# Attention and FFN block for one core: the order of all engines from attention step 14 on written out, O of four half batches turned into SBUF, O transposed held twice

## What is computed

```python
x = L0_attn_x                                   # (16, 256, 256)
xn = _layernorm(x, axis=-1)
x = x + _L0_attn_ref(xn, w_qkv, w_out) + _L0_ffn_ref(xn, w_gating, w_linear)

# attention: 16 heads of 16, causal
q, k, v = (qkv[:, :, 0], qkv[:, :, 1], qkv[:, :, 2])
scores = jnp.einsum('bqhd,bkhd->bhqk', q / 4, k)
scores = jnp.where(causal_mask[None, None], scores, NEG)
out = jnp.einsum('bhqk,bkhd->bqhd', jax.nn.softmax(scores, axis=-1), v).reshape(b, s, HIDDEN)
return out @ w_out

# FFN: operands cast to float8 e4m3
activations = jax.nn.gelu(_qdot(x, w_gating[0])) * _qdot(x, w_gating[1])
return _qdot(activations, w_linear)
```

## Time and profile before

| | us |
|---|---|
| median of 3 runs | 353.13 |
| lowest, highest | 351.51, 353.25 |
| the profiled execution | 353.16 |
| its span (first to last instruction) | 351.4 |

### The profile page before, as it was taken

One profiled execution on the slowest core, in us unless ns is written; L12 is line 12 of the kernel. 1 busy time (PEld: TensorE's weight loads), 2 busy tenths in 40 slices (PEclk: granted clock), 3 DMA queues, 4 the chain that ended last, 5 costly groups with the idle time before them and its releaser, 6 DMA issues.

```text
span 351.4 us, 9794 instructions
## 1 busy us (share of the span) xinstructions
PE 336.0 (96%) x3514; PEld 256.4 (73%) x3514; DVE 294.4 (84%) x1359; ACT 227.4 (65%) x369; POOL 167.6 (48%) x203
## 2 busy tenths in 40 slices
PE   6899999999999999999999999999999999996996
PEld 6446556666676778788888888888888888884775
DVE  5798898989425787999999999899999999999865
ACT  1585677767655576676667766767667666775470
POOL 4114314422225364456675466664755657557461
PEclk9999999999999999999999999999999999999899
DMA  7949975673238243534528346274364552624011
GB/s 239 351 133 294 268 217 156 142 245 122 78 134 298 94 151 109 199 114 161 181 94 270 115 160 209 100 239 158 118 211 136 199 179 97 213 90 157 2 64 60
DMA packets 46569, 57.59 MB, mean 164 GB/s; under 512 B 2680, under 2 KB 39096, under 8 KB 46520
## 3 DMA queue, kind: packets, MB, share of 16 engines
q1 hardware_dynamic: 46520, 56.96, 50.1%
HBM read 16.78 MB, written 12.58 MB: 84 GB/s over the span
## 4 chain that ended last, share of the span: by engine, by line
PE 81%; DVE 9%; DMA 4%; ACT 2%; issue 2%; SPq 1%; DVEq 0%; ACTq 0%
PE ps L954 13%; PE ps L845 13%; PE ps L932 11%; PE ps L905 9%; PE ps L852 7%; PE ps L832 7%; PE ps L975 6%; PE ps L809 6%; PE ps L815 6%; DVE masked L531 4%; DMA xres<-in_L_attn_x_dram 3%; PE ps L963 2%; PE ps L792 2%; DMA xt_store<-stack 1%; ACT gate L618 1%
## 5 line engine op out<-in xcount | busy, mean ns | idle before, releaser
L531 DVE CUSTOM_DVE_ANT_0 masked<-ps,causal 128x256 bf16<-128x256 f32 (+1 forms) x512 | 148.2, 353 | 17.0 <-PE ps L905 17.0
L663 ACT ACTIVATE arena<-ps 128x1024 f32<-128x1024 f32 x96 | 98.3, 1027 | 54.5 <-PE ps L932 54.2
L366 POOL TENSOR_SCALAR_AFFINE_SELECT arena<-arena 128x512 f32<-128x512 f32 (+1 forms) x96 | 73.8, 790 | 32.6 <-ACT arena L663 32.5
L337 POOL TENSOR_TENSOR qk_part<-w_raw,qk_part 128x512 fp32r<-128x512 f32 x32 | 41.2, 1287 | 52.0 <-ACT qk_part L642 52.0
L618 ACT ACTIVATE gate<-ps 128x512 bf16<-128x512 f32 x64 | 38.4, 603 | 27.9 <-PE ps L809 27.7
L932 PE MATMUL ps<-stack 64*128 64x256 f32 (+1 forms) x512 | 51.2, 300 | 2.3 <-ACT arena L663 2.2
L845 PE MATMUL ps<-xs,wq_part 128*128 128x256 f32 x384 | 52.3, 285 | 0.3 <-ACT w_raw L636 0.3
L954 PE MATMUL ps<-arena,v_aug 128*32 128x256 f32 (+1 forms) x1024 | 49.5, 335 | 1.7 <-DVE o_norm L548 1.7
L905 PE MATMUL ps<-stack 63*128 63x256 f32 (+1 forms) x512 | 47.7, 285 | 2.0 <-DVE row_max L531 1.8
L845 PEld LDWEIGHTS ps<-xs,wq_part 128*128 128x128 f32 x384 | 47.5, 189 | 1.5 <-ACT w_raw L636 0.6
L932 PEld LDWEIGHTS ps<-stack 64*128 64x128 f32 x512 | 35.9, 186 | 15.0 <-issue 5.7
(11 more groups left out here) (64 smaller groups left out, 453.1 us busy)
## 6 DMA issues: line engine op xcount, KB each, us to landing
stack<-qk_part SPq DMA_DIRECT2D x96, 256.0 KB, 2.8
xs<-xt_store SPq DMA_DIRECT2D x16, 512.0 KB, 4.4
xt_store<-xt_part SPq DMA_DIRECT2D x14, 512.0 KB, 4.2
out_dram<-w_raw SPq DMA_DIRECT2D x15, 256.0 KB, 4.4
xres<-in_L_attn_x_dram SPq DMA_DIRECT2D x7, 512.0 KB, 6.7
arena<-in_L_ffn_w_gating_dram SPq DMA_DIRECT2D x2, 1024.0 KB, 10.3
stack<-zeros SPq DMA_DIRECT2D x4, 512.0 KB, 7.6
arena<-in_L_ffn_w_linear_dram SPq DMA_DIRECT2D x1, 1024.0 KB, 14.3
```

Of the source, the lines that this page charges most:

```text
L337: nc.gpsimd.tensor_tensor(qk_part[:, g, QLO:KLO + 1:3, :], qk_raw[:, g, :, :], qk_part[:, g, QHI:KLO, :].bitcast(F32), ALU.subtract).then_ ...
L366: nc.gpsimd.affine_select(diag, diag, pattern=[[0, 1024 // width], [1, P]], compare_op=ALU.is_ge, fill=0.0, base=0, channel_multiplier=-1) ...
L531: last = nc.vector.tensor_tensor_reduce(masked[:, place, i * width:(i + 1) * width], max_ps[:, place, i * width:(i + 1) * width], causal[: ...
L663: nc.scalar.activation(arena[:, n, :, :], exp_banks(b, n), ACT.Exp).then_inc(exp_done, 1)
```

## The change

From step 14 on, no engine's order comes from the loop any more; all of them are written out, instruction group by instruction group. With that come four smaller edits:

- `o_to_rows` of the four half batches (12,1), (13,0), (13,1) and (14,0) writes into SBUF (`o_by_q`, on the place of the FFN's weights `wg8`, done with by then) and not back into the bank; `normalize_o` then reads it there, and the next `times_v` waits only for `o_to_rows` and not for the multiply of `normalize_o`.
- `ot_part` is held twice, by the batch's parity, so `round_ot` waits for a `project_out` two batches back and not one.
- Batch 14's output projection and transposed maxima use the other bank of `misc`.
- `keep_warm` of 4 goes, that of 12 becomes 8 and writes another bank. DVE's last subtraction (L597) comes before `add_x(14)` and not after.

No work is added or removed otherwise. The diff, with the lists of SP, POOL and ACT cut short:

```diff
+        o_by_q = wg8[:, :, :, :].rearrange("p g k n -> p (g k n)").bitcast(F32).rearrange("p (c n) -> p c n", c=2)
         ot_raw = xn[:, 2:4, :]
         o_norm = sb("o_norm", [P, S], F32)
-        ot_part = xt_part[:, :, :, 0:S]
+        ot_part = [xt_part[:, :, :, i * S:(i + 1) * S] for i in range(2)]
...
-            return misc[:, 1, :] if b == B - 1 else misc[:, 1 - c, :]
+            return misc[:, 1, :] if b >= B - 2 else misc[:, 1 - c, :]
-            return exp_ps[:, t, 0:D] if b == B - 1 else misc[:, 0, t * D:(t + 1) * D]
+            return exp_ps[:, t, 0:D] if b == B - 1 else misc[:, int(b == B - 2), t * D:(t + 1) * D]
+        def leaves_bank(b, c):
+            return -7 <= 2 * (b - B) + c <= -4
...
-            for s in range(B + 5):
+            for s in range(B - 2):
...
+            place_max(B - 1, 1)
+            store_y(B - 5)
+            store_y(B - 3)
+            store_y(B - 4)
+            store_y(B - 2)
+            store_y(B - 1)
...
-                nc.gpsimd.tensor_tensor(ot_part[:, 1, c, :], ot_raw[:, c, :], ot_part[:, 0, c, :].bitcast(F32),
+                nc.gpsimd.tensor_tensor(ot_part[b % 2][:, 1, c, :], ot_raw[:, c, :], ot_part[b % 2][:, 0, c, :].bitcast(F32),
...
+            mask(B - 1, 4)
+            mask(B - 1, 5)
+            split_ot(B - 2, 0)
             split_ot(B - 2, 1)
             split_ot(B - 1, 0)
...
+                if leaves_bank(b, c):
+                    dve.wait_ge(o_norm_done, 2 * b + c - 1)
+                nc.vector.transpose(o_by_q[:, c, :] if leaves_bank(b, c) else pv_bank(b, c), pv_bank(b, c)).then_inc(o_by_q_done, 1)
             def normalize_o(b, c):
                 done = 2 * b + c + 1
-                o = pv_bank(b, c).rearrange("p (k e) -> p k e", e=2 * DH)
+                o = (o_by_q[:, c, :] if leaves_bank(b, c) else pv_bank(b, c)).rearrange("p (k e) -> p k e", e=2 * DH)
...
-                nc.vector.tensor_tensor(y[b % 2][:, :, :], misc[:, 0, :].rearrange("p (t d) -> p t d", t=QT),
+                nc.vector.tensor_tensor(y[b % 2][:, :, :], misc[:, int(b == B - 2), :].rearrange("p (t d) -> p t d", t=QT),
...
+            find_max(B - 3, 5)
+            o_to_rows(B - 4, 0)
+            find_max(B - 2, 0)
+            find_max(B - 2, 1)
+            normalize_o(B - 4, 0)
+            find_max(B - 2, 2)
+            o_to_rows(B - 4, 1)
+            find_max(B - 2, 3)
+            normalize_o(B - 4, 1)
+            find_max(B - 2, 4)
+            find_max(B - 2, 5)
+            o_to_rows(B - 3, 0)
+            find_max(B - 1, 0)
+            find_max(B - 1, 1)
+            add_x(B - 5)
+            find_max(B - 1, 2)
+            o_to_rows(B - 3, 1)
+            find_max(B - 1, 3)
+            find_max(B - 1, 4)
             find_max(B - 1, 5)
+            normalize_o(B - 3, 0)
             o_to_rows(B - 2, 0)
+            add_x(B - 4)
+            normalize_o(B - 3, 1)
             normalize_o(B - 2, 0)
-            add_x(B - 3)
             o_to_rows(B - 2, 1)
             normalize_o(B - 2, 1)
-            for c in range(2):
-                o_to_rows(B - 1, c)
-                normalize_o(B - 1, c)
+            o_to_rows(B - 1, 0)
+            add_x(B - 3)
+            normalize_o(B - 1, 0)
+            o_to_rows(B - 1, 1)
+            normalize_o(B - 1, 1)
+            dve.wait_ge(ot_hi, 2 * B)
+            nc.vector.tensor_tensor(ot_part[1][:, 1, 1, :], ot_raw[:, 1, :], ot_part[1][:, 0, 1, :].bitcast(F32), ALU.subtract).then_inc(ot_lo_last, 1)
             add_x(B - 2)
-            dve.wait_ge(ot_hi, 2 * B)
-            nc.vector.tensor_tensor(ot_part[:, 1, 1, :], ot_raw[:, 1, :], ot_part[:, 0, 1, :].bitcast(F32), ALU.subtract).then_inc(ot_lo_last, 1)
...
-                if b == 0:
+                if b < 2:
                     act.wait_ge(xt_stored, 16 * B)
                 else:
-                    act.wait_ge(ot_used, 2 * b + c - 1)
-                nc.scalar.copy(ot_part[:, 0, c, :], ot_raw[:, c, :]).then_inc(ot_hi, 1)
+                    act.wait_ge(ot_used, 2 * b + c - 3)
+                nc.scalar.copy(ot_part[b % 2][:, 0, c, :], ot_raw[:, c, :]).then_inc(ot_hi, 1)
...
+            round_ot(B - 5, 1)
+            exponent(B - 3, 0)
...
+            exponent(B - 1, 5)
             round_ot(B - 2, 0)
...
+                elif b >= 1 and leaves_bank(b - 1 + c, 1 - c):
+                    pe.wait_ge(o_by_q_done, 2 * b + c)
...
-            for s in range(2, B):
+            for s in range(2, B - 2):
...
-            exp_scores(B - 1, 0)
-            pe.wait_ge(y_done, B - 3)
-            project_out(B - 3, 0)
+            max_scores(B - 2, 0)
+            exp_scores(B - 3, 0)
+            pe.wait_ge(y_done, B - 5)
+            transpose_max(B - 3, 1)
+            max_scores(B - 2, 1)
+            exp_scores(B - 3, 1)
+            pe.wait_ge(qk_copied[0], B)
+            project_qk(B - 1, 1)
+            max_scores(B - 2, 2)
+            exp_scores(B - 3, 2)
+            times_v(B - 4, 1)
+            max_scores(B - 2, 3)
+            exp_scores(B - 3, 3)
+            pe.wait_ge(qk_copied[1], B)
+            transpose_max(B - 2, 0)
+            pe.wait_ge(neg_done[1], B - 2)
+            project_v(B - 1)
+            exp_scores(B - 3, 4)
+            max_scores(B - 2, 4)
+            times_v(B - 3, 0)
+            max_scores(B - 2, 5)
+            exp_scores(B - 3, 5)
+            pe.wait_ge(v_done, B)
+            project_out(B - 5, 0)
+            max_scores(B - 1, 0)
+            exp_scores(B - 2, 0)
+            project_out(B - 5, 1)
+            pe.wait_ge(neg_done[0], B - 1)
+            transpose_max(B - 2, 1)
+            max_scores(B - 1, 1)
+            exp_scores(B - 2, 1)
+            max_scores(B - 1, 2)
+            exp_scores(B - 2, 2)
+            times_v(B - 3, 1)
+            max_scores(B - 1, 3)
+            exp_scores(B - 2, 3)
+            pe.wait_ge(neg_done[1], B - 1)
+            transpose_max(B - 1, 0)
+            pe.wait_ge(y_done, B - 4)
+            project_out(B - 4, 0)
+            max_scores(B - 1, 4)
+            exp_scores(B - 2, 4)
+            max_scores(B - 1, 5)
+            exp_scores(B - 2, 5)
+            times_v(B - 2, 0)
             pe.wait_ge(neg_done[0], B)
             transpose_max(B - 1, 1)
-            project_out(B - 3, 1)
+            exp_scores(B - 1, 0)
+            project_out(B - 4, 1)
             exp_scores(B - 1, 1)
             exp_scores(B - 1, 2)
             times_v(B - 2, 1)
-            for n in range(3, UNITS):
-                exp_scores(B - 1, n)
+            exp_scores(B - 1, 3)
+            exp_scores(B - 1, 4)
+            pe.wait_ge(y_done, B - 3)
+            project_out(B - 3, 0)
+            exp_scores(B - 1, 5)
             times_v(B - 1, 0)
-            pe.wait_ge(y_done, B - 2)
+            project_out(B - 3, 1)
+            times_v(B - 1, 1)
+            pe.wait_ge(neg_done[1], B)
             project_out(B - 2, 0)
-            keep_warm(4, misc[:, 1, :])
-            times_v(B - 1, 1)
             project_out(B - 2, 1)
             pe.wait_ge(exp_done, UNITS * B)
             project_out(B - 1, 0)
-            keep_warm(12, misc[:, 1, :])
+            keep_warm(8, max_ps[:, 0, :])
             project_out(B - 1, 1)
```

87 lines of the change are left out of this document (67 added, 20 removed).

## The result

The changed kernel takes 349.04 us (median of 4 runs, 348.36 to 349.12), beside it the kernel before 353.19 us (median of 4, 351.51 to 355.06). The ratio is 0.9877, 95% between 0.9836 and 0.9919: faster by 1.2%, 4.15 us. The forecast was 348.4, in a range from 346.9 to 351.0. The profiled execution took 349.11 us, with a span of 347.4 us where it was 351.4.

The account below looks back on a forecast made before the run. PE paces the loop to step 14, then idles 4.5 us for ACT, the multiply and find_max. Saving 2.7 waits, 1.3 low clock, 1.3 work, giving back 0.5 at the end: 353.16 less 4.8, 348.4 us; range 346.9 to 351.0.

Parts of the forecast that it names:

- Low clock: Before the last times_v: the 1.3 us that a times_v lost at the 1.2 GHz level would be saved.
- Work that leaves the stretch: Before the last times_v: project_out(14,0), 0.8 us, and four warming matmuls, 0.5 us, leave PE's list; 1.3 us saved.
- Waits: From step 14 to the last times_v: PE's waits shrink by 2.7 us, 1.6 of them for the multiply.
- stalls (3) and (4): PE waits for DVE's find_max before max(15,2), 0.86 us, and before max(15,5), 0.84 us.
- Stall (2): In step 14, exp(13,1) waits 0.19 us for the exponent of exp(13,0).
- (5): In step 15, exp(15,1) waits 0.43 us for exponent (15,0), and exp(15,5) 0.12 us for exponent (15,3).
- the multiplies wait for POOL: Rival, chance 0.09: multiplies reading SBUF wait for POOL, 1.2 us on the first, some on the last; 349.6 to 350.
- The clock falls again: Rival, chance 0.15: PE's clock falls once around two stalls in step 15, costing 1.3 us; 349.7 us.
- DVE and ACT faster: Rival, chance 0.07: both engines beat the reckoning in the tail, so stalls (3) and (4) go; 346.8 us.
- The gain doesn't come: Rival, chance 0.08: the tail's old waits only change names, its pace set by exp, exponent, exp; 352 to 353 us.
- the ring of exponents: In the tail: exp, exponent, exp with one pair of banks, 1.5 us a unit, 18 units, 27 us of 32.
- Slower: Rival, chance 0.06: the clock falls before max(15,2) and stays low as stalls repeat every 4 or 5 us; 355 us.

Follow-up runs that it names:

- the warming run: The kernel before, with 8 matmuls nobody reads added at each of PE's two waits in step 15; 351.71 us, ratio 0.9957.
- the last kernel: The changed kernel with exp(15,0) before transpose_max(15,1), exponent (15,0) before negate_max(15,1), and 5 warming matmuls at the end instead of 8; 348.43 us, ratio to before 0.9893.

## Why the prediction was right, point by point

**The bound and the place: right.** Step 14 begins where it did, and the whole difference lies behind it.

**The sum of the parts.** From 305.29 to the last `times_v` 37.80 us were to become 32.5, and became 338.64 - 305.31 = 33.33. The end was to give back 0.5 us and gave back 4.88 - 4.49 = 0.4. So 4.1 instead of 4.8 us. By its three terms:

- *Low clock, 1.3 us*: right, by the warming run.
- *Work that leaves the stretch, 1.3 us*: nothing speaks against it; it is in the lists, not in a measurement of its own.
- *Waits, 2.7 us*: this is the term that was too large, by 0.8 us. The waits that the view counts came as forecast, 4.5 us up to the last `times_v` before and 1.8 now, with stalls (3) and (4) at 321.66 and 327.46 (forecast 321.60 and 327.27). The step that failed is the pricing of what stands around them, and it is found by subtracting the loop's prices from start to start:
  - `exp(14,2)` and `exp(14,5)` come 0.14 us late each, for the exponents shown above. Stall (2) was found by just this reckoning (exponent at 306.46, `exp(13,1)` at 307.54); for these two I left it out.
  - `transpose_max(14,1)` and `(15,1)` take 0.31 us each, where I took 0.13 from the earlier trace rows. There projections stand behind it; here scores do. The view counts no wait there. With the projection behind `transpose_max(15,1)`, in the last kernel, it takes 0.13 again. Why, no run shows.
  - The unit ahead of a `times_v` takes 0.43 instead of 0.34 three times (322.14, 327.94, 335.87), and `project_out` up to 0.90 instead of 0.84; with smaller pieces this makes 0.6. Why, no run shows.

  That is 1.2 us. Against it the stalls (3) and (4) are 0.70 us each and not 0.86 and 0.84, and two small waits of (5) came 0.1 short in all, so part of the error cancelled. A unit behind a wait is not dearer by itself: in the kernel with the new order and O in PSUM, `exp(14,5)` starts 0.34 us after a unit that waited 0.79 us, since there the exponent, begun at 326.81, was ready by 327.88.

```profile
327.56 0.50 PE L998 MATMUL ps<-stack 63*128 63x256 f32 x4 [0.79 <-DVE row_max L574]
327.90 0.50 PE L1025 MATMUL ps<-stack 64*128 64x256 f32 x4
```

  So `exp(15,0)` came at 330.12 where 329.5 was forecast, and the last `project_out` at 343.52 where 342.8 was.

How well the total came out hangs also on where it was counted from: an execution of before with a mean clock of 0.995, like 22 of the 39. The 1.3 us of low clock are a saving only beside such an execution.

**What brings the waits down: half wrong.** I wrote that `o_to_rows` into SBUF takes away the 1.6 us for the multiply. It does, and two runs show that this alone brings nothing: the same time comes back as waits for `find_max`. DVE is the engine behind both. The 1.85 to 2.0 us come from DVE's list, in which the normalising moves behind the last maxima; O in SBUF is only what permits it.

**The price no row showed: wrong in size, right in effect.** I took nothing for the multiplies from SBUF. They cost 0.9 us of DVE time in all (0.52 + 0.82 + 0.63 + 0.58 less 4 × 0.42), and by my own sign, a multiply of 0.8 us or more, the step was wrong. That the sum still held was due to the slack that I named: with the masks gone the last `times_v` comes no earlier. The rival *the multiplies wait for POOL* was right on its mechanism and wrong on its price. `o_to_rows` itself costs nothing in SBUF: 0.71 us, beside 0.73.

**The other engines: right.** POOL and PE were to be level at the last mask: the masks end at 336.21 + 2.27 = 338.48, PE goes on at 338.64. `normalize_o(14,0)` transposes at 334.50 and `normalize_o(15,0)` at 340.10, both without a wait, `add_x(14)` at 343.20 too, and `project_out(15,0)` waits 0.18 for its split, for which I had 0.2.

**The rivals.** *The clock falls again*: it did not in the changed kernel (0.999 or 1.00 in eight executions); with O in PSUM it did in one of ten. *DVE and ACT faster*: no, both stalls are there, 0.70 us each. *The gain doesn't come*: it came for O in SBUF without the new DVE list, by the mechanism named (waits change their name), though through DVE and not through the ring of exponents. The ring itself cost the changed kernel the two times 0.14 us above. *Slower*: its mechanism was seen there too, a clock that stays low, at a smaller price: 1.7 us of tail, about 1.1 of them by the clock.

## What to carry to other kernels

A wait that names a producer is only worth something if that engine has something else to do first: look what stands next in its list, and whether PE will wait for that instead. Giving a buffer free early pays through the reordering that it allows, so the two are to be weighed together, and the move of an operand from PSUM to SBUF is to be charged with what it meets on POOL wherever no slack follows. When one stall moves, work out anew what every unit behind it waits for, also where the view of waits shows no idle time; and take the price of a unit from a row that has the same neighbour behind it.

## What the runs showed of the hardware

- A multiply of 128x256 with both operands in SBUF took from 0.42 us (POOL idle) to 1.28 us (beside a POOL addition of 128x512), and 1.045 us on the mean of 29; with one operand in PSUM it took 0.42 us throughout. POOL lost too: its addition of 128x512 went from 1287 to 1353 ns on the mean, its mask of 128x1024 from 1094 to 1168, while its mask of 128x512 stayed at 0.63 to 0.64 us on the mean; the one beside the multiply of 0.82 us in the changed kernel took 0.82.
- The granted clock fell with some clusters of waits and not with others. It fell to 0.50 behind waits of 0.95 and 1.12 us that ended at 321.33 and 323.18. It stayed at 1.00 with waits of 0.63 and 0.64 us, ended at 321.66 and 327.46 (changed kernel), and also with 0.89, 0.77 and 0.96 us, ended at 324.25, 327.84 and 331.08 (new order, O in SBUF, normalised early):

```profile
330.00:332.00 2.00, 1.03 (x16) 0.66 (x11) 1.93 (x9) 0.37 (x1) 1.03 (x2) 1.00 0.02 4
```

  Where the line runs between these, the runs don't tell, and the kernel doesn't settle it alone: the mean clock of the kernel before was 0.998 or more in 8 of 39 executions and 0.985 in 9. Eight matmuls of 128x128 in each wait held the clock up in all ten executions.
- The way from `negate_max` through its DMA to the next exponent matmul is short in the tail: begun at 330.25 in the last kernel, it let `exp(15,3)` start at 332.51 without a wait, 2.3 us at most.
